# Pairwise products of 32 fields: W moved into the first transfer, the head's loads reordered and the output slots cut anew

## What is computed

```python
def _L0_rec_ref(x, W):                      # x: 4096 x 32 x 64, W: 64 x 64, float32
    vid = jnp.einsum('bfd,de->bfe', x, W)
    F_ = x.shape[1]
    idx_i, idx_j = jnp.triu_indices(F_, k=1)
    return x[:, idx_i, :] * vid[:, idx_j, :]   # 4096 x 496 x 64
```

## Time and profile before

| | us |
|---|---|
| median of 3 runs | 1284.16 |
| lowest and highest | 1283.9, 1284.31 |
| the profiled execution | 1284.14 |
| its span in the trace | 1282.6 |
| VectorE busy | 1080.3 (84%) |
| TensorE busy, 256 matmul instructions | 179.8 (14%) |
| moved by DMA | 553.73 MB, 432 GB/s over the span |

### The profile page before, as it was taken

The page is one execution under the profiler, slowest core; times in us unless marked ns, Lnnn a source line. Parts: engine busy times, 40 slices in busy tenths (PEclk is TensorE's granted clock), DMA queues, the critical chain, the costliest instruction groups (busy, mean ns, idle before and its releaser), DMA issues. The chain is left out here.

```text
span 1282.6 us, 1142 instructions
## 1 busy us (share of the span) xinstructions
PE 179.8 (14%) x256; PEld 70.4 (5%) x256; DVE 1080.3 (84%) x292; POOL 0.2 (0%) x4
## 2 busy tenths in 40 slices
PE   3011040304010031012111201002212030111000
PEld 1000010101000010000000000001000010000000
DVE  5898999999996456989999998483898999899971
POOL 0000000000000000000000000000000000000000
PEclk7655565755565565565565656556557565565555
DMA  9999999999999999999999999999999999999999
GB/s 421 419 441 437 425 442 426 441 421 439 444 413 450 417 437 439 429 441 423 435 421 433 432 456 417 435 416 434 450 433 425 425 456 427 425 444 437 427 425 409
DMA packets 11090, 553.73 MB, mean 432 GB/s; under 512 B 1232, under 2 KB 1360, under 8 KB 1360
## 3 DMA queue, kind: packets, MB, share of 16 engines
q1 hardware_dynamic: 10080, 524.82, 94.7%
q10 hardware_dynamic: 1008, 28.90, 5.3%
HBM read 33.62 MB, written 520.09 MB: 432 GB/s over the span
## 5 line engine op out<-in xcount | busy, mean ns | idle before, releaser
L173 DVE TENSOR_TENSOR mem<-mem,vid 128x1024 f32<-128x1024 f32 (+11 forms) x292 | 1080.3, 3770 | 174.8 <-DMA out_dram<-mem 144.4
L237 PE MATMUL vid<-mem,w 128*128 (+1 forms) x256 | 179.8, 870 | 1004.8 <-PEq L236 1004.8
L237 PEld LDWEIGHTS vid<-mem,w 128*128 128x128 f32 x256 | 70.4, 289 | 1113.4 <-issue 1113.4
L339 POOL MEMSET const-bfloat16-1.0<- 128x1 bf16 x1 | 0.1, 102 | 0.0
L339 POOL MEMSET const-uint8-127<- 128x1 uint8 x1 | 0.1, 102 | 0.0
L339 POOL MEMSET const-float32-0.0<- 128x1 f32 x1 | 0.1, 99 | 0.2 <-issue 0.2
L339 POOL MEMSET const-float32-1.0<- 128x1 f32 x1 | 0.1, 99 | 0.0
## 6 DMA issues: line engine op xcount, KB each, us to landing
out_dram<-mem SPq DMA_DIRECT2D x11, 7680.0 KB, 31.0
out_dram<-mem SPq DMA_DIRECT2D x11, 7168.0 KB, 23.1
out_dram<-mem SPq DMA_DIRECT2D x8, 6656.0 KB, 21.9
out_dram<-mem SPq DMA_DIRECT2D x4, 6144.0 KB, 24.2
out_dram<-mem SPq DMA_DIRECT2D x2, 5120.0 KB, 20.7
out_dram<-mem ACTq DMA_DIRECT2D x1, 7680.0 KB, 27.4
mem<-in_r_x_dram SPq DMA_DIRECT2D x2, 2048.0 KB, 60.5
out_dram<-mem SPq DMA_DIRECT2D x1, 3072.0 KB, 20.5
```

Source lines behind the costliest of these rows:

```text
L173: self.engine.tensor_tensor(*operands, MULT).then_inc(self.dve, 1)
L237: nc.tensor.matmul(vid[:, b * BANK : b * BANK + BANK, :], lhsT=w2, rhs=mem[:, bass.ds(k * step + (first + b * BANK), BANK), :], start=True ...
L339: nc = _bacc.Bacc("TRN2", target_bir_lowering=False, num_devices=1, dynamic_dma_scratch_size=256)
```

## The change

W becomes a field of the first transfer: `mem` and W are now parts of one SBUF tensor, W at field 0 of it and `mem` behind it, and the host lays W ahead of the 16 first fields of tile 0 in one array, so one transfer of 17 fields takes the place of x0 and W. Tile 0 now lies at field 0 and tiles 1 to 5 at 286 to 477 (the arithmetic of `WALKS`), so the head is: 16 fields at 16 (the second half of tile 0), 128 fields at 286 (tiles 1 to 4), 32 fields at 414 (tile 5). Tiles 6 to 10 are loaded to 32 to 159 and 0 to 31, tiles 11 to 15 to 286 to 445, behind slots 23 and 44. The list has 67 slots with other sizes and places, and other cuts. The first store isn't held; after a stretch the hold stays as it was. Counted from the code, 280 products take the place of 292; what is computed, and the bytes moved, are the same.

```diff
-WALKS = [(range(5), 286, 32), (range(5, 6), 0, 32), (range(6, 11), 286, 32), (range(11, 16), 128, -32)]
+WALKS = [(range(1), 0, 32), (range(1, 6), 286, 32), (range(6, 11), 128, -32), (range(11, 16), 286, 32)]
 PLACE = [first + step * k for tiles, first, step in WALKS for k in range(len(tiles))]
-HEAD = range(6), [(302, 128), (0, 32), (430, 16)]
+HEAD = range(6), [(16, 16), (286, 128), (414, 32)]
 STRETCHES = [
-    (range(6, 11), [(286, 128), (414, 32)]),
-    (range(11, 16), [(32, 128), (0, 32)]),
+    (range(6, 11), [(32, 128), (0, 32)]),
+    (range(11, 16), [(286, 128), (414, 32)]),
 ]
 SLOTS = [
-    (120, 32), (112, 174), (96, 32), (80, 128), (104, 208), (120, 32), (128, 184), (104, 32),
...
-    (128, 176), (128, 310), (128, 64), (128, 192), (128, 32), (120, 320),
+    (120, 32), (128, 158), (80, 32), (104, 112), (64, 222), (120, 32), (128, 158), (128, 16),
+    (128, 144), (128, 0), (128, 128), (112, 0), (112, 112), (120, 224), (104, 0), (128, 104),
...
+    (128, 0), (112, 128), (128, 262), (128, 0), (120, 128),
 ]
 CUTS = {
-    3: (46,), 6: (24,), 11: (64,), 17: (110,), 21: (6,), 28: (24,), 36: (112,), 40: (120,),
...
+    3: (46,), 5: (80,), 6: (64,), 7: (16,), 8: (14,), 10: (16,), 15: (120,), 18: (104,),
...
 }
-LOAD_BEHIND = [24, 45]
+LOAD_BEHIND = [23, 44]
-def build(nc, x0, x, w, out):
-    mem = nc.alloc_sbuf_tensor("mem", [P, UNITS, C], F32).ap()
-    w2 = nc.alloc_sbuf_tensor("w2", [P, P], F32).ap()
+def build(nc, x0, x, out):
+    whole = nc.alloc_sbuf_tensor("mem", [P, 1 + UNITS, C], F32).ap()
+    w, mem = whole[:, 0, :], whole[:, 1:, :]
-    a = PLACE[0]
-    load(act, mem[:, a : a + HALF, :], x0[:, :HALF, :], "x0", [(0, f) for f in range(HALF)])
-    ws = load(act, w2, w, "w", [])
+    ws = load(act, whole[:, : 1 + HALF, :], x0[:, : 1 + HALF, :], "x0", [(0, f) for f in range(HALF)])
-    held = stretch(act, *HEAD, "h")[-2], 16
+    stretch(act, *HEAD, "h")
+    held = None
-                    lhsT=w2,
+                    lhsT=w,
-    x0 = _np.pad(x[:, 0, :HALF], ((0, 0), (0, PAD0), (0, 0)))
+    x0 = _np.concatenate([w2[:, None], x[:, 0, :HALF]], 1)
+    x0 = _np.pad(x0, ((0, 0), (0, PAD0), (0, 0)))
```

More of the change, by code:

```diff
@@ L37 @@
 SLOTS = [
[9 rows of a table removed]
[9 rows of a table added]
 ]
 CUTS = {
-    3: (46,), 6: (24,), 11: (64,), 17: (110,), 21: (6,), 28: (24,), 36: (112,), 40: (120,),
-    47: (14,), 52: (30,), 53: (24,), 54: (16,), 55: (30,), 57: (48,), 59: (112,), 61: (32,),
-    64: (112,), 65: (118,), 66: (32,),
[3 rows of a table added]
 }
-LOAD_BEHIND = [24, 45]
+LOAD_BEHIND = [23, 44]
 SP_SLOTS = len(SLOTS) - 2
@@ L343 @@
     x = x.reshape(2, NT, C, F, D).transpose(0, 4, 1, 3, 2).reshape(P, NT, F, C)
-    x0 = _np.pad(x[:, 0, :HALF], ((0, 0), (0, PAD0), (0, 0)))
-    order = [t * F + f for tiles, runs in (HEAD, *STRETCHES) for lo, n in runs for t, f in fields(tiles, lo, n)]
-    x = _np.pad(x.reshape(P, NT * F, C)[:, order], ((0, 0), (0, PAD), (0, 0)))
     w2 = _np.zeros((P, P), _np.float32)
@@ L349 @@
     w2[D:, D:] = w
+    x0 = _np.concatenate([w2[:, None], x[:, 0, :HALF]], 1)
+    x0 = _np.pad(x0, ((0, 0), (0, PAD0), (0, 0)))
+    order = [t * F + f for tiles, runs in (HEAD, *STRETCHES) for lo, n in runs for t, f in fields(tiles, lo, n)]
+    x = _np.pad(x.reshape(P, NT * F, C)[:, order], ((0, 0), (0, PAD), (0, 0)))
     arrays, args = {}, []
-    for name, a in zip((_INS[0] + "_0", *_INS), (x0, x, w2)):
+    for name, a in zip((_INS[1] + "_x0", _INS[0]), (x0, x)):
         a = _np.ascontiguousarray(a)
```

## The result

The changed kernel takes 1286.95 us (median of 14 runs, 1285.06 to 1287.74), the kernel before 1284.41 (14 runs beside them, 1283.89 to 1284.83): 1.0019 times as long, 95% interval 1.0012 to 1.0027. It is 2.5 us slower, and the interval doesn't reach 1; 1284.0 was forecast and the range ended at 1286.2. Its runs also lie further apart: 2.7 us between the fastest and the slowest, against 0.9 before.

A forecast was written before the change was run, and what follows sets the result against it. The prediction took the 16 DMA engines' transfers, busy throughout, as the bound. From 1284.14 us before, it took -0.1 for two fewer transfers and 0 for the other parts, giving 1284.0 us, range 1283.0 to 1286.2.

The forecast's parts named there:

- The bound, and what is around it: Whole kernel: the 16 DMA engines' transfers set the time, 8449 fields at 0.1513 us; VectorE does not.
- W inside, two transfers fewer: Head and slot list: each transfer costs 0 to 0.1 us beyond its bytes, so two fewer give -0.1 us.
- rival (c): All transfers: each costs its own time in series, about 2.0 us, so the sum would be 1280; chance 0.02.
- The head's order: Head, tile 0's second 16 fields: VectorE's 1.40 us wait goes but becomes a longer wait for a store; worth 0.
- The first store not held: Head: store 0 goes 2.2 us earlier beside the last load; taken as 0, with 3.2 us kept for the range.
- The row that the zero was taken from: Stores of ACT's and SP's queues at 1242 to 1246, said to alternate with the pace staying 0.1513 us a field.
- Rival (a): Head: up to 0.8 us for each of 3 or 4 load/store turns, 1286.4 to 1287.2; chance 0.13.
- Places and slots: All 67 slots: stores are issued early enough, 2.1 us or more spare everywhere, engines never dry; cost 0.
- the two lines: Hand-carried times through all 67 slots: VectorE filling each slot, and stores landing 0.151 us a field behind the one ahead.
- The need: Least time from a store's issue to the landing ahead: 1 us to first byte plus about 0.5, 1.5 us.
- The rival (d): Up to ten slots: engines run dry because VectorE is slower beside the traffic; 1 us each is +10, 1294; chance 0.03.

## Why the prediction was wrong

**The bound, and what is around it: right.** Transfers set the time, and what was lost is, within some tenths, the time in which the engines had none.

**W inside, two transfers fewer (-0.1): not contradicted.** The run with W apart can't tell 0.1 from none; it rules out the 2 us of rival (c).

**The head's order (0): right.** The wait of 1.40 went and turned into waits for stores. TensorE's first half tile took from 6.02 to about 12.2, longer than before (5.20 us from 6.29), so VectorE began at 12.22 and not at 11.4 and SP issued store 0 at 28.72; nothing hung on it.

**The first store not held (0, at most 3.2): not free, but small by itself.** Alone it costs 0.4 us or nothing. The picture behind it was wrong: in the profiled execution no load packet came after a store packet, so there was no turn to pay for; load packets beside the issued store took longer, 0.6 us an engine. The row that the zero was taken from the earlier trace rows is no such case: by the packets from 1242 to 1246, each engine began ACT's store only when its last data packet of SP's was done. And it left the engines up to 2 us apart, for which the sum had no term: landings and issues were compared as if the 16 engines were one. By the medians, holding the store is worth 1.2 us with the waits ahead and 1285.12 - 1284.64 = 0.5 with the waits home (1.0 and 0.4 from the kernels before beside them). Rival (a) had 1286.4 to 1287.2, and the measured 1286.95 lies in it by luck: two waits moved home take 2.0 of the 2.5 us away with the head left as it is.

**Places and slots (0): this is the step that failed.** It said that 2.1 us or more were spare everywhere and that the engines don't run dry. The distances themselves were good: for the store near 1046 (slot 54) the two lines gave 3.8, for the one near 256 (slot 13), which the prediction doesn't name, they give about 4.2, and with the two waits home the trace has 4.2 and 3.9. They were wrong for the kernel as it is, since the lines let every product wait only for what it needs. The text ahead of the prediction says that `Products.emit` puts waits ahead of their products, and the working left it out. Its price is in the changed kernel's rows: VectorE's 3.16 and 3.57 us. Of the distances, 4.2 - 1.5 = 2.7 and 3.8 - 1.5 = 2.3 were spare; the excess of 0.5 and 1.3 became 1.3 and 1.5 us of idle engines. The need was itself put too low: adding the mean idle time to the distance at the places that ran dry gives 0.2 + 1.5 near 1046 and, in the other versions' traces, 1.6 to 1.9 where the engines are at most 1 us apart, but 0.9 + 1.3 = 2.2 near 256, where they are 1.9 apart. (The places were misread once more, without effect: tiles 1 to 5 lie at fields 286 to 445, since `mem` ends at 446, and not to 477.) The rival (d) named the right effect (dry engines) for a wrong reason (a slower VectorE, at up to ten slots), and so put a chance of 3 in 100 and 1294 us on it.

**The bounds.** The upper end, 1286.2, took in half of (a) and none of (d). A term with a sharp edge, where nothing is lost until the spare distance is used up, deserved the range it has on both sides of the edge.

What stays open: the 0.4 to 0.8 us that every version without dry engines has over the kernel before (1284.64, 1284.64 and 1284.66 against 1284.2, and 0.66, 0.63 and 0.79 in the others). Each is within its interval of none, and no run told where they would come from.

## What to carry to other kernels

Where transfers are the bound and hold a queue, count the distance from each issue to the end of the transfer ahead, and count it with the waits where the program really puts them, not where they are needed. A wait that is moved ahead is free as long as the distance is long and costs all of its excess where it isn't; the sum of waits on the page tells nothing of that. Compare the first engine's end with the last one's landing, since a spread among the engines is taken off the distance too. And give the awaited work the range of its own time: the same half tile took from 5.1 to 6.8 us in these traces, and at a place without spare distance that goes into the total.

## What the runs showed of the hardware

- A store into an empty queue has its first packets 0.8 us after its issue (256.40 to 257.2 and 1046.74 to 1047.6).
- Where a store of one queue was issued beside the last load of another, the load's packets took up to 1.55 us on some engines and the usual 0.61 on others: 1.9 us between first and last engine in the profiled execution of the changed kernel, 0.8 to 2.1 in others with the same head. The spread lasts for hundreds of us. It ends where all engines have to wait for one store (from 1.9 at 257 to 0.2 at 275), and without such a place it shrinks slowly (from 2.1 at 50 to 1.3 at 419 with both waits home).
- TensorE's half tile of the same eight instructions took 5.09 us at a granted clock of 0.72 and 6.16 at 0.59, both after some 53 us without work.
- A kernel with short distances takes different times from run to run: 2.7 us between the fastest and slowest of 14, against 0.9 before. The spread of the head can't be all of it, since with the first store held and the waits ahead the runs still lie 2.2 us apart; TensorE's time at the two places is the other candidate, and no run here separates them.
- Two stretches' turns from stores to loads cost what they did before: their packets took 0.9 and 0.8 us an engine over the steady pace before, 0.8 and 0.7 after.
